# Earlier small transfers, folded context weights, diagonal values, one bank for narrow keys and values, and more copies on ScalarE, in a four-layer diffusion transformer

## The reference, cut to what matters

```python
ctx = text_embed @ W_ctx + b_ctx          # layer 1
k = _heads(ctx @ W_k)
v = _heads(ctx @ W_v)
...
kv = brain_tokens @ cond_w.T + cond_b     # layer 3
k = _heads(kv @ wk.T + bk, H)
v = _heads(kv @ wv.T + bv, H)
attn = jax.nn.softmax(jnp.einsum('bhqd,bhkd->bhqk', q, k) * scale, axis=-1)
```

## Time and profile before

| | |
|---|---|
| time before, median of 3 runs | 1553.26 us (1553.22 to 1553.7) |
| profiled execution, its own time | 1552.47 us |
| its span, first to last instruction | 1550.5 us |
| TensorE busy / VectorE busy | 1418.2 us (91%) / 1369.5 us (88%) |
| ScalarE busy / GpSimd busy | 1084.1 us (70%) / 912.4 us (59%) |
| mean granted TensorE clock | 0.987 |

### The profile page before, as it was taken

One profiled execution on the slowest core, in us unless ns is written; L12 is line 12 of the kernel. 1 busy time (PEld: TensorE's weight loads), 2 busy tenths in 40 slices (PEclk: granted clock), 3 DMA queues, 4 the chain that ended last, 5 costly groups with the idle time before them and its releaser, 6 DMA issues.

```text
span 1550.5 us, 40860 instructions
## 1 busy us (share of the span) xinstructions
PE 1418.2 (91%) x15228; PEld 1179.1 (76%) x15228; DVE 1369.5 (88%) x3746; ACT 1084.1 (70%) x4757; POOL 912.4 (59%) x1028
## 2 busy tenths in 40 slices
PE   3999989999889999999999999898999999999887
PEld 3888867778777788777777787676778887788754
DVE  5876988898999998888999989999899799998887
ACT  0486797776866776868777475774877878776753
POOL 3675765454665666665556556676656555555553
PEclk9999999999999999999999999999999999999989
DMA  8300000000000000000000000000000000000000
GB/s 282 123 2 2 2 2 2 2 2 1 2 7 8 6 8 3 2 1 2 2 6 8 3 6 8 3 6 9 2 2 2 2 2 2 1 2 4 3 3 6
DMA packets 14870, 20.91 MB, mean 13 GB/s; under 512 B 4113, under 2 KB 11089, under 8 KB 14673
## 3 DMA queue, kind: packets, MB, share of 16 engines
q1 hardware_dynamic: 13520, 14.77, 3.0%
q10 hardware_dynamic: 1152, 3.54, 0.6%
HBM read 17.25 MB, written 1.05 MB: 12 GB/s over the span
## 4 chain that ended last, share of the span: by engine, by line
PE 54%; DVE 30%; ACT 12%; POOL 2%; issue 1%; DMA 1%; SPq 0%; DVEq 0%; ACTq 0%; POOLq 0%
PE ps L740 12%; DVE negmax L1218 9%; PE ps L858 9%; ACT E L947 9%; PE ps L756 6%; PE ps L884 5%; DVE E L1324 5%; PE ps L898 5%; PE ps L766 4%; PE ps L835 3%; PE ps L821 2%; PE ps L909 2%; PE ps L871 2%; DVE E L1276 2%; POOL E L1062 1%; PE ps L848 1%
## 5 line engine op out<-in xcount | busy, mean ns | idle before, releaser
L947 ACT ACTIVATE E<-ps,negmax 128x128 f32<-128x128 f32 x2048 | 723.3, 426 | 125.9 <-DVE negmax L1218 116.1
L1062 POOL TENSOR_TENSOR E<-E,rinv 128x512 f32<-128x512 f32 x512 | 528.6, 1046 | 284.7 <-DVE rinv L1227 279.8
L947 ACT ACTIVATION_READ_ACCUMULATOR E<-ps,negmax 128x1 f32 x2048 | 538.9, 267 | 0.0
L1218 DVE TENSOR_REDUCE negmax<-ps 128x4 f32<-128x512 f32 x512 | 325.2, 679 | 31.3 <-PE ps L821 16.7
L858 PE MATMUL ps<-consts,E 128*128 128x128 f32 x2048 | 295.1, 278 | 27.1 <-POOL E L1062 12.1
L1324 DVE COPY E<-ps 128x512 f32<-128x512 f32 x448 | 296.3, 678 | 21.1 <-PE ps L858 18.9
L858 PEld LDWEIGHTS ps<-consts,E 128*128 128x128 f32 x2048 | 231.3, 142 | 89.2 <-POOL E L1062 43.9
L956 ACT ACTIVATE VV<-ps 128x512 f32<-128x512 f32 x128 | 78.0, 620 | 180.3 <-PE ps L756 179.8
L1055 POOL TENSOR_TENSOR E<-E,prod 128x512 f32<-128x512 f32 x128 | 162.5, 1275 | 62.3 <-DVE prod L1279 54.7
L1008 POOL TENSOR_TENSOR rstd<-ve,consts 128x1 f32<-128x1 f32 (+1 forms) x192 | 108.6, 568 | 70.3 <-DVE ve L1171 61.3
L884 PE MATMUL ps<-E,VV 128*64 128x128 f32 x2048 | 131.1, 278 | 9.9 <-ACT E L947 5.3
(11 more groups left out here) (134 smaller groups left out, 2679.6 us busy)
## 6 DMA issues: line engine op xcount, KB each, us to landing
w_f<-res_f SPq DMA_DIRECT2D x6, 256.0 KB, 9.8
E<-in_x SPq DMA_DIRECT2D x16, 64.0 KB, 1.8
w_cq<-res_cq SPq DMA_DIRECT2D x2, 512.0 KB, 7.3
w_co<-res_co SPq DMA_DIRECT2D x2, 512.0 KB, 10.2
w_f<-res_f SPq DMA_DIRECT2D x2, 512.0 KB, 9.3
out_x<-X SPq DMA_DIRECT2D x16, 64.0 KB, 1.5
rows<-in_rows SPq DMA_DIRECT2D x1, 832.0 KB, 10.1
E<-in_ctx SPq DMA_DIRECT2D x16, 48.0 KB, 3.0
```

The source lines that it names most:

```text
L947: last = nc.scalar.activation(E[p][:, h, :], bank(u, j * N, (j + 1) * N), ACT.Exp, bias=negmax[p][:, h:h + 1], accum_out=sums[p][:, h:h + 1])
L1062: tt(e, e, rinv[p][:, T4 * g:T4 * g + T4].unsqueeze(2).broadcast_to([N, T4, N]), ALU.mult).then_inc(done[POOL], 1)
L1218: nc.vector.tensor_reduce(negmax[p][:, T4 * g:T4 * g + T4], bank(u).rearrange("p (h m) -> p h m", h=T4), AX, ALU.max, negate=True).then_in ...
```

## The change

It has five parts, and the order of all steps is planned anew with other priorities.

1. **Transfers.** The first 129 columns of the constants and `lnc` are issued by ScalarE, ahead of its weights. SyncE's order is condition, x and context of sample 0, vectors, the one row of `rows` that block 0 adds (128 columns), sample 1, the rotary tables alone (384 columns), samples 2 to 5, the weights of block 1, the other twelve rows, and so on; the transposed contexts come after that, and `colmask` is gone. Waits follow: the vectors, the first row, the rotary tables and `lnc` have semaphores of their own.
2. **Folded contexts.** Once for block 4 and once for block 10, TensorE multiplies the context matrix into the key and value weights (step "FOLD", a 96 x 256 product and two one-column products for the biases) and VectorE writes the result over the weights. Keys and values then come straight from the transposed context. The step "C" is gone, 32 times on TensorE and 32 times on VectorE.
3. **Diagonal values.** Step "V" copies 128 elements per partition into their places (128x4x4x8) where a 128x512 product with the mask stood. The zeros around them are written by GpSimd (step "zero", a memset of 128x512) in blocks 3 and 9, 32 times; blocks 4 and 10 find them still there.
4. **One bank.** Keys and values of blocks 3, 4 and 10 are filled by one TensorE step "KV" in one bank.
5. **ScalarE copies.** It takes group 3's transposed weights in all small blocks (`turns_on`) and Q0 and K0 in flat blocks (`copies_heads`), 64 copies each of 128x512.

```diff
-AGE = 16.8
-TURN = [0, 0, 0, 0, 0, 0, 0, 0, -3, 0, 1, 0, -2, 0, 0, 20]
-AHEAD = {"flat": 1.6}
+AGE = 18.2
+TURN = [0, 0, -6, -4, 2, -1, 0, -3, -3, -6, 1, 0, -1, 0, 0, 21]
+AHEAD = {"flat": 14.1, "rope": 2.5, "small": 5.9}
+LEAN = {PE: 0.0, DVE: 0.00061, ACTE: 0.00295, POOL: 0.00053}
...
-                score = (start, -rank[key], index[key])
+                score = (start + 0.0 - LEAN[e] * rank[key], -rank[key], index[key])
...
+def copies_heads(n):
+    return ACTE if n in ("Q0", "K0") else DVE
...
-    return ACTE if KIND[b] == "rope" and g % 2 else DVE
+    return ACTE if KIND[b] == "rope" and g % 2 or KIND[b] == "small" and g == 3 else DVE
...
             sp.dma_start(condT[:, :], cond_t).then_inc(cond_loaded, 16)
-            sp.dma_start(V[:, :], vecs).then_inc(cond_loaded, 16)
             load(0)
-            sp.dma_start(C[:, 0:NFIRST], consts[:, 0:NFIRST]).then_inc(consts_first_loaded, 16)
-            sp.dma_start(LNC[:, :], lnc).then_inc(consts_first_loaded, 16)
+            sp.dma_start(V[:, :], vecs).then_inc(vecs_loaded, 16)
+            sp.dma_start(R[:, 0:D], rows[0:D].partition_broadcast(128)).then_inc(row_first_loaded, 16)
             load(1)
-            sp.dma_start(C[:, NFIRST:], consts[:, NFIRST:]).then_inc(consts_loaded, 16)
-            load(2)
-            sp.dma_start(R[:, :], rows.partition_broadcast(128)).then_inc(rows_loaded, 16)
+            sp.dma_start(C[:, NFIRST:NROPE], consts[:, NFIRST:NROPE]).then_inc(rope_loaded, 16)
...
-                elif step == "C":
...
-                    mm(bank(u, 0, N), wt[:, :], ctxT[p][:, :],
-                       start=True, stop=True).then_inc(done[PE], 1)
+                elif step == "FOLD":
+                    wt, of_ctx = weights("cqkv1" if b == 4 else "cqkv3"), weights("ctx1" if b == 4 else "cond3")
+                    vacated()
+                    mm(ps[0:CD, u[0], 0:2 * D], of_ctx[:, :], wt[:, D:3 * D], start=True, stop=True)
...
+                            mm(bank(u, 0, N), wt[0:rows, D:2 * D], src[:, :], start=True, stop=True)
+                            mm(bank(u, N, 2 * N), src[:, :], wt[0:rows, 2 * D:3 * D], start=True, stop=True)\
...
+                elif step in ("Q0", "Q1", "K0", "K1"):
+                    g = GROUP[step]
+                    nc.scalar.activation(E[p][:, T4 * g:T4 * g + T4, :], bank(u).rearrange("p (t n) -> p t n", t=T4),
...
+            act.dma_start(C[:, 0:NFIRST], consts[:, 0:NFIRST]).then_inc(consts_first_loaded, 16)
             act.dma_start(stage["mod_first"], setup_w["mod_first"]).then_inc(mod_first_loaded, 16)
+            act.dma_start(LNC[:, :], lnc).then_inc(lnc_loaded, 16)
...
+                elif step == "zero":
...
+                    nc.gpsimd.memset(VV[p][:, 0:T4 * D], 0.0).then_inc(done[POOL], 1)
...
-                    tt(vmask[p], bank(u, 0, D).unsqueeze(1).broadcast_to([N, T4, D]),
-                       c("colmask").rearrange("p (r f) -> p r f", r=T4), ALU.mult).then_inc(done[DVE], 1)
...
+                    nc.vector.tensor_copy(own_features[p], bank(u, at, at + D).rearrange("p (j r e) -> p r j e", r=T4, e=HD))\
+                        .then_inc(done[DVE], 1)
```

More of the change, by code:

```diff
@@ new lines @@
+    (DVE, "U0", "ff"): -88, (DVE, "V", "small"): -4, (DVE, "VAR", "small"): 22, (DVE, "aggr", "small"): 4,
+    (DVE, "factors", "small"): 46, (DVE, "heads", "small"): -64, (DVE, "max", "rope"): -8, (DVE, "norm", "ff"): 4,
+    (DVE, "norm", "rope"): -12, (DVE, "rcp", "rope"): -18, (DVE, "rcp", "small"): 4, (DVE, "squares", "small"): -2,
+    (DVE, "stats", "flat"): 100, (DVE, "stats", "small"): 16, (DVE, "sum", "ff"): -4, (DVE, "sum", "flat"): 102,
+    (DVE, "sum", "rope"): 4, (DVE, "sum", "small"): 8}
@@ L656, in set_up @@
             def set_up():
-                pe.wait_ge(cond_loaded, 32)
-                for _ in range(WARMING):
-                    mm(ps[0:len(VEC), BANKS - 1, 0:len(VEC)], V[:, :], V[:, :], start=True, stop=True)
-                pe.wait_ge(consts_first_loaded, 32)
+                pe.wait_ge(cond_loaded, 16)
+                pe.wait_ge(consts_first_loaded, 16)
             def step_of(step, b, s):
@@ L812, in step_of @@
                     else:
-                        for by, count in latest_first(*[EMPTY[UNIT[b, s, n]] for n in "QK"]):
+                        for by, read in ((DVE, "K"), (ACTE, "Q")):
+                            count = DONE[by, read, b, s]
                             if fresh(pe, done[by], count):
```

193 lines of the change are left out of this document (118 added, 75 removed).

## The result

The changed kernel takes 1530.19 us (median of 4 runs, 1529.7 to 1532.15), the kernel before 1553.48 beside it: a ratio of 0.9851 (0.9838 to 0.9865; an interval behind a ratio is its 95% interval), 23 us faster. 1495 had been predicted, a gain of 58: the direction was right, the gain far too large. The profiled execution took 1532.15 us, its span 1530.1.

The account below looks back on a forecast made before the run. TensorE and VectorE, both nearly full, were taken to bound the kernel together, neither alone. Behind the start -47 us (between -31 by chain shares and -63), start -9, together -56: 1496.5, settled at 1495 from about 1553; range 1458 to 1532.

Parts of the forecast that it names:

- I put the norm at 11, so 9 us are gained.: Start: sample 0's first norm on VectorE at 11 us instead of 20.00, through the new transfer order; 9 us gained.
- VectorE's work: together -119.: VectorE: shorter value copies, no context copies, copies moved to ScalarE; 119 of 1369.5 us busy time removed, 8.7%.
- An engine's work is then worth about its share on the chain.: Whole kernel: work priced by share of the last-ending chain: TensorE 54%, VectorE 30%, ScalarE 12%; -31 us behind the start.
- The upper bound: if TensorE is fed as well as in its best stretch: From 60 to 1450 us, TensorE at 97.56% throughout: 1331 us for 1390, -59; with the end -63.
- I take the middle: Behind the start: -47 us, taken between the chain-share sum of -31 and the upper bound of -63.
- If the waiting stays as it is.: Condition on the chain-share sum of -31 us for everything behind the start.
- ScalarE +13 and TensorE -4: By chain shares: ScalarE's 74 us of added work costs 13 us, TensorE's 6 us of removed work gains 4.
- The rival of ScalarE's queue: ScalarE's 128 new copies wait behind exponentials and hold up TensorE, 0.7 us each: cost 90, time 1587; 5%.
- The folds and GpSimd at nothing: Folds' wait for weights costed at nothing (about 2 us work per engine, once); GpSimd's 32 memsets, 16 us, hidden.
- TensorE alone: Rival: TensorE alone is the bound, VectorE's relief worth nothing in the middle; -20 us, 1533; 17%.
- the sign named for it: TensorE's share in the middle stays near 94%, where the forecast had 95% to 96% from 50 to 1400 us.
- VectorE alone: Rival: VectorE alone is the bound, so its 119 us come back in full, limited by TensorE's work to 1447; 18%.

Follow-up runs that it names:

- the last experiment: Changed kernel with planner numbers fitted further, x and context of samples 1 and 2 issued ahead of first row and rotary tables, order unchanged: ratio 0.9714, 1510.07 us.
- b_dve_less: Kernel before, order unchanged, VectorE's value product and some copies cut short (73.7 us less busy, part of the computation left out): ratio 0.9932, worth 10.6 us.
- the best order of the old steps: Kernel before with its planner numbers fitted further by 14 minutes of random search; steps, transfers and engines unchanged: ratio 0.9854, 1530.6 us.
- the nudged kernel before: Kernel before with the planner's AGE at 16.95 in place of 16.8 and nothing else: ratio 1.0174, 1580.3 us.

## Why the prediction was right or wrong, point by point

**"I put the norm at 11, so 9 us are gained."** The power did wait for the variance alone, as said, but the norm came at 13.54, past the bound of 12.4. (The prediction gave two values for that bound, 12.4 and 13.9, and took the gain of 6 from the second; 6.5 was measured.) The wait was named and its length was wrong: sample 1's context was there at 13.17, not near 10. Issued ahead of the first row it was there at 10.47, in the last experiment. The second wait of the same kind, for sample 2 with hT behind it, was overlooked. The term was 3.6 us by the first projection and 4.2 by its own run; the last experiment, where both waits shrink and the projection comes 3.8 us earlier still, shows them as the cause.

**"VectorE's work: together -119."** Measured: -87.3. The parts were right by duration. The values' copy with its runs of 8 took 276 ns for the 281 assumed. But a busy time is a union and durations overlap: in the rotation that follows the first projection one instruction of 0.68 us starts at 23.04 and the next at 23.64. Over all of VectorE the durations add up to 1609.5 us before and 1499.4 after, 110 less, while the busy time fell by 87: some 23 us of the -119 were never busy time. Another 10 went to the norms (mean 435 ns for 381), below.

**"An engine's work is then worth about its share on the chain."** This is the step that failed. It gave 0.34 us for each of VectorE's, 0.59 for TensorE's and 0.17 for ScalarE's. In a fixed order 0.14, 0.29 and 0.04 were paid (0.10 and 0.31 for the first two on the changed kernel). As we read it, the chain names the last of several things that were nearly ready together; take it away and the next is a little earlier. By the paid rates and the measured busy times the prediction's sum would have been 4.2 + 0.14 x 87 - 0.04 x 56 = 14 us, an estimate, where it had 56.

**"The upper bound: if TensorE is fed as well as in its best stretch", and "I take the middle".** TensorE went from 93.8% to 94.6% in the middle, nowhere near 97.6%. Nothing on record showed that VectorE's room was what fed TensorE in its best stretch, and VectorE's relief did not spread that state. This choice alone added 16 us to the forecast.

**"If the waiting stays as it is."** The condition was written down and not priced. The order was planned anew with other tables, and at the same work that moved the time by 18 to 23 us down and by 27 to 52 up. The prediction's sum has no term for it. The single terms that were measured in a fixed order make 15 of the 23; the rest came with the new plan or with the parts not run alone. The planner's number was no part of the prediction; read beside it, it would have said -22.1.

**ScalarE +13 and TensorE -4.** ScalarE's busy time rose by 55.7, not by 74. In the trace the durations of its copies out of PSUM add up to 78 us more and those of its table loads to 9 less, as reckoned, but its exponentials with their sums are 15 shorter in total, which no term had. In an order that wasn't fitted the kernel with the copies on ScalarE was 19 us slower than the one without, in a fitted one 17 faster. Neither sign can be read from busy times. The rival of ScalarE's queue (1587) is close to the changed steps under the old tables (1582), but that those lost by the mechanism it named is not shown; with the fitted order the loss isn't there. TensorE's busy time changed by -0.8.

**The folds and GpSimd at nothing.** The profile agrees: no idle time stands before the folds' products, and the 32 memsets of 528 ns, 16.9 us, fit in GpSimd's idle time. No run took either out alone.

**The rivals.** 1530 lies nearest to "TensorE alone" (1533), and the sign named for it came: TensorE's share in the middle stayed near 94% (94.6%). Its number is near by luck. TensorE is not the bound alone: 53 us less of its work paid 15.5, not 70. The rival's sum had 9 for the start (4.2 measured), 6 for TensorE's own work (0.8 of busy time) and 4 to 7 for VectorE's relief, which was worth 10.6 over the whole kernel. And 1530 lies within the forecast's range only because the range was drawn out to this rival's case. "VectorE alone" (1447) fell with b_dve_less. The Trainium skill's page "Perfetto Trace Analysis", section "Identifying the Most-Contended Engine", spoke for that rival: by its share of weight loads, TensorE is at 76% and VectorE the fullest engine. The runs disagree: for each us of busy time, relief of TensorE paid twice that of VectorE.

## What to carry to other kernels

When a planner or a table sets the order, take the tables for a part of the change of their own: nudge them first, and see by how much the time moves at unchanged work. Here that was 27 to 35 us, more than the change; compare two versions only at equal fit, and look at the granted clock of each. Don't take a share of the chain as a price: in this kernel, where engines hand work to each other in fixed queues, relief of TensorE, VectorE or ScalarE paid a half to a quarter of it. At a start, list what each engine's fixed order waits for one by one, for the second and third sample too.

## What the runs showed of the hardware

TensorE's busy time is no measure of work. The same 15228 records took 1410.6 us in the best order of the old steps and 1449.5 in the worst, the old steps under the new tables; the mean granted clock was 0.989 in the first and 0.970 in the second, and groups that stand alone last longer per record. By the clocks alone 1410.6 would become 1438 us, an estimate (x 0.989/0.970), so most of the 39 us goes with the clock. A worse order does not always lower it: the nudged kernel before was at 0.985. And it is no property of the order alone: ten executions of one order (changed steps, old tables, copies on VectorE) were granted 0.971 to 0.987 and took 1549.77 to 1568.65 us.

Beside GpSimd's work a norm from SBUF on VectorE lasted up to 1.40 us, four times its median of 0.34. Two rows of the changed kernel in order of time, start and length:

```profile
259.18 1.22 DVE L1234 TENSOR_SCALAR xn<-X,mv,rstd 128x128 f32<-128x128 f32 x1
259.28 1.04 POOL L1117 TENSOR_TENSOR E<-E,rinv 128x512 f32<-128x512 f32 x1
```

The norm's row starts 0.10 us ahead of the product's and still ends behind it. Of the 192 norms, 134 with GpSimd idle at their start lasted 0.358 us in the mean, 36 that began during a product L1117 0.654 and 7 that began during a product L1110 0.904. Only 5 overlap a memset, with 0.34 to 0.75 us. The Trainium skill's page "SBUF — State Buffer", section "Who interferes with whom", says that GpSimd and VectorE share a pair of ports; this trace agrees. But the part that it was weighed against, the memsets, cost about 1 us by it at most, and the longer norms come mainly from products that were there before too and met them more often in the new order: 43 norms began during one, for 29 before.

A VectorE copy from PSUM that writes 128 elements per partition in runs of 8 is as fast (276 ns) as one to contiguous places (281 ns).
